# First graph's pass: TensorE's last two aggregations of a chunk put in front of the next chunk's first and second query and its second placing

## The reference, cut to what matters

```python
Q = (h @ Wq).reshape(n, H, HD)
K = (h @ Wk).reshape(n, H, HD)
V = (h @ Wv).reshape(n, H, HD)
score = jnp.einsum('ehd,ehd->eh', K[src], Q[dst]) / np.sqrt(HD) + edge_bias
m = jax.ops.segment_max(score, dst, num_segments=n)
ex = jnp.exp(score - m[dst])
denom = jax.ops.segment_sum(ex, dst, num_segments=n)
attn = ex / denom[dst]
out = jax.ops.segment_sum(attn[:, :, None] * V[src], dst, num_segments=n)
```

## Time and profile before

| | |
|---|---|
| time, 3 runs | 5411.74 us median (5407.52 to 5449.04) |
| profiled execution | span 5404.7 us from its first to its last instruction |
| first graph's pass | about 245 to 1870 us of the span, 55 chunks |
| there, per 300 us (600 to 900) | DVE busy 248, PE 219, POOL 187, ACT 118 us |
| mean granted TensorE clock | 0.85 of 2.4 GHz |

### The profile page before, as it was taken

One profiled execution on the slowest core, in us unless ns is written; L12 is line 12 of the kernel. 1 busy time (PEld: TensorE's weight loads), 2 busy tenths in 40 slices (PEclk: granted clock), 3 DMA queues, 4 the chain that ended last, 5 costly groups with the idle time before them and its releaser, 6 DMA issues. The chain is left out here.

```text
span 5404.7 us, 69347 instructions
## 1 busy us (share of the span) xinstructions
PE 3933.5 (73%) x16281; PEld 2847.1 (53%) x16282; DVE 3064.0 (57%) x7623; ACT 1859.8 (34%) x5073; POOL 2464.9 (46%) x2442
## 2 busy tenths in 40 slices
PE   6867777777777659967853666666666338999999
PEld 4545555555555448856732444444444226777776
DVE  3278887878888766662154666666667773111111
ACT  1333333333333312311222444444444322333332
POOL 2256665656666450001166666666663422333332
PEclk8988988888888879977986788777887559999999
DMA  2555555555555232211173333333331451111111
GB/s 80 186 146 149 154 151 148 151 140 153 147 148 151 83 118 84 91 55 40 52 252 89 95 96 96 94 95 94 93 96 47 127 194 20 32 32 31 31 31 27
DMA packets 316127, 553.64 MB, mean 102 GB/s; under 512 B 63431, under 2 KB 213783, under 8 KB 315857
## 3 DMA queue, kind: packets, MB, share of 16 engines
q0 software_dynamic: 137120, 388.63, 27.4%
q1 hardware_dynamic: 178736, 161.98, 9.8%
HBM read 459.75 MB, written 90.62 MB: 102 GB/s over the span
## 5 line engine op out<-in xcount | busy, mean ns | idle before, releaser
L427 POOL DMA_INDIRECT attend_ring<-kv_rows,all_step_src x880 | 860.1, 977 | 624.5 <-PE attend_ps_agg L468 371.3
L931 POOL DMA_INDIRECT edge_ring<-head_rows,all_step_src x880 | 878.7, 999 | 457.1 <-issue 204.2
L967 PE MATMUL edge_ps_agg<-edge_msg,edge_sel 128*128 128x264 f32 x1760 | 676.3, 520 | 188.9 <-issue 57.3
L468 PE MATMUL attend_ps_agg<-attend_msg,attend_sel 128*128 128x264 f32 x1760 | 605.1, 445 | 179.7 <-DVE graph_qa L785 122.9
L967 PEld LDWEIGHTS edge_ps_agg<-edge_msg,edge_sel 128*128 128x128 f32 x1760 | 414.5, 257 | 328.2 <-issue 198.7
L1266 DVE TENSOR_TENSOR graph_acc<-graph_acc,edge_ps_agg 128x264 f32 x880 | 369.9, 420 | 367.2 <-PE edge_ps_agg L967 169.0
L2821 DVE TENSOR_TENSOR moe_gl<-moe_ps_h,moe_act 128x341 f32<-128x341 f32 x210 | 107.8, 514 | 776.8 <-PE moe_ps_h L2739 776.8
L452 PE MATMUL attend_ps_q<-graph_qa,attend_sel_t 128*128 x1760 | 527.7, 429 | 27.4 <-ACT attend_sel_t L581 17.8
L785 DVE SCALAR_TENSOR_TENSOR graph_qa<-graph_qa,all_step_same,attend_ps_agg 128x264 f32 x880 | 421.1, 479 | 170.1 <-remote 121.0
L468 PEld LDWEIGHTS attend_ps_agg<-attend_msg,attend_sel 128*128 128x128 f32 x1760 | 329.3, 208 | 347.2 <-issue 148.6
L2739 PE MATMUL moe_ps_h<-experts_w,moe_xt 128*128 x1680 | 501.7, 451 | 0.6 <-ACT moe_xt L2770 0.6
(11 more groups left out here) (424 smaller groups left out, 6587.9 us busy)
## 6 DMA issues: line engine op xcount, KB each, us to landing
attend_ring<-kv_rows,all_step_src POOLq DMA_INDIRECT x880
edge_ring<-head_rows,all_step_src POOLq DMA_INDIRECT x880
kv_rows<-qkv_kv SPq DMA_DIRECT2D x25, 512.0 KB, 2.9
experts_w<-in_w_t SPq DMA_DIRECT2D x16, 682.0 KB
attend_mask<-run_starts SPq DMA_DIRECT2D x440, 8.1 KB
edge_mask<-run_starts SPq DMA_DIRECT2D x440, 8.1 KB
head_rows<-hds_hh SPq DMA_DIRECT2D x25, 264.0 KB
qkv_x<-in_x SPq DMA_DIRECT2D x25, 256.0 KB, 3.3
```

Of the source, the lines that this page charges most:

```text
L427: nc.gpsimd.indirect_dma_start(ring[:, step % RING1, :], None, g.kv_rows, bass.IndirectOffsetOnAxis(g.step_src[:, step:step + 1], 0)).then ...
L468: nc.tensor.matmul(ps_agg[i % SUM_BANKS][:, 0:AGG], sel[:, q % 2, u % QU, :], msg[:, q % 2, u % QU, :], start=True, stop=True).then_inc(s_ ...
L931: nc.gpsimd.indirect_dma_start(ring[:, n % slots, u, :], None, g.head_rows, bass.IndirectOffsetOnAxis(g.step_src[:, step:step + 1], 0)).th ...
L967: nc.tensor.matmul(ps_agg[i % BANKS][:, 0:AGG], sel[:, q % 2, u % QU, :], msg[:, q % 2, u % QU, :], start=True, stop=True).then_inc(s_agg, 1)
```

## The change

In PE's `turn` the calls at its end are put in another order. Aggregation 14 now stands in front of the next chunk's first query, aggregation 15 and `at_node` behind that query, and the second placing and the second query come last. No other engine's order changes, and nothing is added or taken away.

```diff
                 if b is not None:
                     add_up(b, 12, 13)
-                if after:
-                    query(c + 1, 0, ahead)
-                    place_t(c + 1, 1)
                 if b is not None:
                     add_up(b, 14)
                 if after:
-                    query(c + 1, 1, ahead)
+                    query(c + 1, 0, ahead)
                 if b is not None:
                     add_up(b, 15)
                 if a is not None:
                     at_node(a)
+                if after:
+                    place_t(c + 1, 1)
+                    query(c + 1, 1, ahead)
                 return ahead
```

## The result

The changed kernel takes **5438.32 us** (median of 20 runs, 5419.64 to 5463.04) where the kernel before takes 5418.0 (20 runs, 5401.16 to 5449.04): ratio **1.0042**, interval 1.003 to 1.0054. The medians are 20 us apart; the ratio makes it some 23 us slower. The profiled execution took 5444.53 us with a span of 5442.6. The forecast was 5500.

The account below looks back on a forecast made before the run. No engine is full; at each first-pass turn's end the chain over ACT and PE was taken to end last. 52 turns x 1.7 us = 88 on span 5404.7 gives 5493, plus 7: 5500 us; range 5345 to 5590.

Parts of the forecast that it names:

- Aggregation 14 ahead of the first query: PE's turn end: starts about 1222.35 instead of 1222.98, some tenths of a us hidden in PE's 2.9 us of idleness.
- Aggregation 15: PE's turn end: ends 1224.38, 5.1 us into the gathers, still late; release about 1226, 0.6 us earlier for DVE.
- the row: POOL's eight gathers without pause at a turn's end; from about 5 us in, PE's finished work was taken as announced late.
- rival 2: Aggregation 15 slips through on time, the first aggregation comes 0.6 us later per turn: 31 us, 5443 us; chance 0.30.
- The placing: Second placing, moved behind aggregation 15 and `at_node` on PE: ends about 1225.0, first aggregation 1.7 us later each turn.
- The third late one: The placing as third late release of the turn's end, a quarter of the way from 1226.6 to 1230.8.
- g: Time at which the second placing is released to ACT: forecast 1227.7, own range 1227.0 to 1229.2; 1225.0 if on time.
- release + 2.81: On ACT and PE, the first aggregation starts 2.81 us after the placing's release: 0.03, 0.60, then 2.18 us.
- DVE is 1.7 us later per turn: L710 follows `row` directly, so the later first aggregation delays DVE 1.7 us in each of 52 turns, 88 us.
- The turned scores: Made on PE; DVE's L700 waits for them until 1230.85 anyway, and the chain over ACT and PE ends last.
- Rival 1: Lateness belongs to a place in PE's order, not the gathers; first aggregation 1.0 us earlier, 83 less, 5329 us; chance 0.20.
- Rival 3: The placing is held until the gathers are over: 4.8 us a turn, 250 us, 5662 us; chance 0.08.

Follow-up runs that it names:

- e3: Kernel before, with POOL's fifth of the eight gathers at a turn's end also waiting for aggregation 15; 5363.02 us, ratio 0.9906.
- e4: Kernel before, with POOL's fifth of the eight gathers at a turn's end also waiting for the turned scores; 5351.93 us, ratio 0.9888.
- f4: Changed kernel, with POOL's fifth of the eight gathers also waiting for the turned scores; 5324.35 us, ratio 0.9816 to the kernel before.
- e7: Kernel before, with one write of zeros on POOL ahead of the fifth gather, on the faster kind of chip; 5028.84 us, ratio 0.9997.
- g1: Kernel before, with one write of zeros on POOL ahead of the fifth gather, on the slower kind of chip; 5467.63 us, ratio 1.0001.
- g3: Changed kernel, with three writes of zeros per turn on POOL, on the slower kind of chip; 5403.91 us, ratio 0.9874 to the kernel before.

## Why the prediction was wrong

*Aggregation 14 ahead of the first query:* right, a few tenths, hidden.

*Aggregation 15:* the start and the end were right to the hundredth (1224.38 worked out, 1240.23 - 15.85 measured). The step failed at its last sentence. "Just late again" at 5.1 us was a guess between an end 3.9 us into the row on time and one 5.65 us in late; the nearest rows left that open. It was on time, and in all turns: L785's wait is 0.6 us. That was rival 2's condition.

*The placing:* here the sum failed. "The third late one", taken a quarter of the way to g = 1227.7, made the first aggregation 1.7 us later in each of 52 turns, and that was the sum's only term. In the turn shown g is 1242.30 - 15.85 = 1226.45, and by "release + 2.81" the first aggregation is due at 1229.26; it came at 1229.11, 0.3 later than before. But in 30 of 51 turns the placing was taken up within 0.52 us of its end, and the median of the first aggregation is 0.9 us earlier in the turn, not 1.7 later. A quarter of the way between two bounds was no measurement.

*The path:* the second step that failed is "DVE is 1.7 us later per turn", by L710's delay, with all behind L710 as it was. L710's wait for `row`, which was to grow, fell from 50.1 to 12.4, and from the row's first gather L710 starts at 14.16 us instead of 14.43. The loss that both pairs of profiles show lies behind it, from L710 to L735: 0.38 to 0.47 us a turn, 20 to 25 us, where 23 were measured; 88 were forecast. The prediction put this stretch at nothing without a reason.

*The turned scores:* this was the decisive place, and I had only half of it. That L700 would not come before the row's end was in the text ("DVE's own gain is lost in that wait"), and so it was: 1230.72 against 1230.85. But I called ACT's chain the last one. In the changed kernel PE often waits for the scans behind L700 instead. The change moved PE's work to where its result was read late.

*Rival 2* gave 5443 us, 5 off, and its condition came true, since aggregation 15 was on time. But it had the first aggregation 0.6 us later in every turn, which the traces don't show: that its number was near is luck.

*Rival 1* (no part for the gathers, 5329) had the first aggregation 1.0 us earlier, and it came 0.9 earlier; the gain did not follow, since DVE stood at L700. It falls by e3, e4 and f4, where only POOL's wait changed. The rule of the Trainium skill named there, "SBUF — State Buffer", section "Who interferes with whom", that a DMA never contends with a compute engine, agrees with the trace of e7 on B, where a release 5.88 us into the gathers had no delay. On A it does not tell what one sees: the turned scores are read up to 4.8 us late while gathers run. No run here shows whether a port has a part in it. *Rival 3* (5662), the placing held to the row's end in every turn, falls with the 30 turns in which it was not late.

*Engines and queues:* at `at_node`, the second query and SP nothing showed. The second pass and the rest differ by 5.7 us of span, which two single executions can't tell from nothing. The range 5345 to 5590 held the time; the chances leaned to the wrong case.

**Shown:** on A, with POOL held idle ahead of the fifth gather, DVE never waits at L700 for the turned scores, and the order of the change gains 0.6% there. **Argued:** that the loss behind L710 comes from PE waiting for the late scans and being at 1.2 GHz afterwards. **Not settled:** what in a row of gathers delays a release on A, and why B has none of it. It isn't POOL's instruction stream alone, since zeros in it did not end the delay.

## What to carry to other kernels

When an engine's result is read late though its record ends early, look what else was running between the two, and measure from that activity's start and end: here the turned scores became readable 1.6 to 1.95 us after the last gather's end, however early PE had made them. Then ask of all turns what one turn shows: the placing's 1.7 us was not the rule, and two profiles of one kernel lay 31 us apart at the last gather of this pass. Moving work ahead of such a wall gains nothing; moving the wall does, even by adding a wait. And a number that falls into the expected range proves only what its rival would have missed: the placing's 2.3% may have in large part a plainer cause, which showed only where nothing was late.

## What the runs showed of the hardware

- The same kernel takes 5416 to 5465 us on some chips and 5031 to 5033 on others, 7 to 8% less, and the two differ in kind. With one kernel file (e7, g1), `row` is read late in none of 22 turns on the second kind and late in 44 of 49 on the first. An edit worth 1.4% on the one (three writes of zeros) is worth 0.0% on the other, so a gain should be measured on both.
- On the first kind, in the changed kernel, aggregation 15 ended 4.2 to 5.4 us after the row's first gather and was on time in all turns but one. The placing right behind it, at 5.4 to 5.6 us in most turns, was on time in 30 of 51 and 1.0 to 5.5 us late in 21. The turned scores, at 6.0 to 7.3 us, were 2.4 to 4.8 us late in all 50 turns in which DVE waited for them, in 47 till 1.6 to 1.95 us after the last gather. No sharp age tells late from on time.
- A write of zeros among the gathers made aggregation 15 less late (its add starts 1.1 us after its end in the median turn of g1, 1.8 in the kernel before), but didn't end the delay: behind a write turned scores were 3.5 us late though the next row was 1.1 us old (g3).
- Between L710 and L735 two turns of one kernel differ by the query's 1.91 us at a granted clock of 0.54 and 1.03 us at 1.00.
